# Forming the low parts of the expert weights on GpSimd, between the transfers of the scatter, instead of on VectorE

## The reference, cut to what matters

```python
scores = sigmoid(xt @ gate_w.T)              # 16 experts, 4 groups, best 2 groups, best 4 experts
combine = one_hot(indices) weighted          # token x expert
h1 = einsum('td,eid->tei', xt, W1)
h3 = einsum('td,eid->tei', xt, W3)
g = silu(h1) * h3 * combine[:, :, None]      # inner width 176
y = einsum('tei,edi->td', g, W2)
z = silu(xt @ Ws1.T) * (xt @ Ws3.T) @ Ws2.T  # shared expert, inner width 352
out = x + gb * (y + z)
```

## Time and profile before

| | us |
|---|---|
| median of 3 runs | 1134.69 |
| the profiled execution | 1135.41 |
| its span | 1133.6 |
| PE busy in the span | 907.7 (80%) |
| DVE busy | 763.4 (67%) |
| POOL busy | 660.5 (58%) |
| ACT busy | 561.1 (49%) |

### The profile page before, as it was taken

One profiled execution on the slowest core, in us unless ns is written; L12 is line 12 of the kernel. 1 busy time (PEld: TensorE's weight loads), 2 busy tenths in 40 slices (PEclk: granted clock), 3 DMA queues, 4 the chain that ended last, 5 costly groups with the idle time before them and its releaser, 6 DMA issues.

```text
span 1133.6 us, 20825 instructions
## 1 busy us (share of the span) xinstructions
PE 907.7 (80%) x6980; PEld 759.1 (67%) x6981; DVE 763.4 (67%) x1637; ACT 561.1 (49%) x1054; POOL 660.5 (58%) x631
## 2 busy tenths in 40 slices
PE   4484899999999999999999974431159899999930
PEld 4462578888788888888888764331149799999920
DVE  5655778878878888788788856560037666666657
ACT  1202477777777777777777851110024344444410
POOL 4421478788787777887877763047720045555544
PEclk9696899999999999999999995565559899999975
DMA  5743251233422334223242106523310133334345
GB/s 169 278 154 81 58 155 43 74 66 69 147 53 73 64 77 132 52 73 64 59 140 44 27 1 223 154 75 117 115 37 1 33 115 112 118 114 121 102 173 197
DMA packets 65105, 112.31 MB, mean 99 GB/s; under 512 B 16848, under 2 KB 41815, under 8 KB 63151
## 3 DMA queue, kind: packets, MB, share of 16 engines
q1 hardware_dynamic: 46950, 76.94, 25.2%
q0 software_dynamic: 6912, 17.84, 4.4%
q10 hardware_dynamic: 11168, 16.52, 4.3%
HBM read 45.86 MB, written 41.16 MB: 77 GB/s over the span
## 4 chain that ended last, share of the span: by engine, by line
PE 70%; DVE 11%; issue 7%; POOL 4%; DMA 3%; another core or an unknown queue 3%; ACT 2%; SPq 0%; POOLq 0%; DVEq 0%; ACTq 0%
PE bank L621 12%; PE bank L623 12%; PE bank L622 12%; PE bank L738 9%; PE bank L761 8%; PE bank L974 6%; PE bank L885 2%; PE bank L855 2%; PE bank L946 2%; POOL p_lo L1741 1%; PE bank L715 1%; PE bank L832 1%; DVE h L1469 1%; DMA rows_f<-turns 1%
## 5 line engine op out<-in xcount | busy, mean ns | idle before, releaser
L1741 POOL TENSOR_TENSOR p_lo<-p_f,p_hi 128x512 f16<-128x512 f32 x256 | 312.8, 1228 | 85.4 <-ACT p_f L1526 82.7
L1523 ACT ACTIVATE p_hi<-bank,log_up 128x512 f16<-128x512 f32 x256 | 176.1, 688 | 134.4 <-PE bank L623 133.8
L1165 DVE TENSOR_REDUCE nmax<-bank 128x1 fp32r<-128x512 f32 x256 | 173.9, 686 | 68.5 <-PE bank L738 65.8
L1526 ACT ACTIVATE p_f<-bank,log_up 128x512 f32<-128x512 f32 x256 | 175.2, 684 | 0.9 <-POOL p_lo L1741 0.9
L738 PE MATMUL bank<-qk 128*128 128x512 f32 x256 | 152.5, 599 | 6.1 <-DVE nmax L1165 3.8
L761 PEld LDWEIGHTS bank<-vals,p_hi 128*128 128x128 f16 x2048 | 109.5, 97 | 59.2 <-POOL p_lo L1741 30.5
L1145 DVE TENSOR_TENSOR qk<-rows_f,qk 128x512 fp32r<-128x512 f32 (+1 forms) x128 | 143.4, 1121 | 2.0
L761 PE MATMUL bank<-vals,p_hi 128*128 128x66 f16 x2048 | 138.6, 194 | 3.2 <-POOL p_lo L1741 3.0
L761 PE MATMUL bank<-vals,p_lo 128*128 128x66 f16 x1024 | 121.0, 193 | 0.0
L1719 POOL TENSOR_TENSOR turns<-turns 128x512 f32<-128x512 f32 x64 | 90.3, 1413 | 47.0 <-DVE turns L1139 47.0
L1794 POOL DMA_INDIRECT slots<-h,slot_i x64 | 62.3, 974 | 70.0 <-DVE slot_i L1355 50.8
(11 more groups left out here) (228 smaller groups left out, 2093.6 us busy)
## 6 DMA issues: line engine op xcount, KB each, us to landing
rows_f<-turns SPq DMA_DIRECT2D x64, 256.0 KB, 3.9
slots<-pad ACTq DMA_DIRECT2D x4, 2880.0 KB, 11.2
h<-slots SPq DMA_DIRECT2D x80, 144.0 KB
w_hi<-parts SPq DMA_DIRECT2D x16, 512.0 KB, 7.6
rows_f<-kl_f SPq DMA_DIRECT2D x32, 192.0 KB, 3.1
w_raw<-in_w SPq DMA_DIRECT2D x4, 1408.0 KB, 10.5
h_dram<-h_hl SPq DMA_DIRECT2D x3, 1024.0 KB, 4.9
qk<-lat_st SPq DMA_DIRECT2D x16, 192.0 KB, 3.5
```

The lines of the kernel that those rows point to most:

```text
L1165: dve.tensor_reduce(nmax[:, k % MAXES:k % MAXES + 1], max_bank[q % 2][:], AX_X, ALU.max, negate=True)\
L1523: act.activation(p_hi[:, u % TB, :], score_bank[u % 2][:], ACT.Exp, bias=log_up[:, 0:1], scale=SCALE)
L1526: act.activation(p_f[:, u % 2, :], score_bank[u % 2][:], ACT.Exp, bias=log_up[:, 0:1], scale=SCALE)\
L1741: pool.tensor_tensor(p_lo[:, u % TB, :], p_f[:, u % 2, :], p_hi[:, u % TB, :], ALU.subtract).then_inc(s_pl, 1)
```

## The change

The subtraction that makes `w_lo` of one expert leaves position t of the shared stage on DVE. It now stands in POOL's scatter loop, once per tile, behind the four transfers of tile t, with a wait for `w_h` of at least t + 2. Semaphore `w_l` is raised by POOL instead of DVE. Its final value and the waits on it are as before. Nothing else differs.

```diff
@@ shared_position on DVE
                     dve.tensor_tensor(zg, y_bank[par][:, 0:D], g2, ALU.mult).then_inc(z_zg, 1)
 
-                    dve.wait_ge(w_h, t + 2)
-                    dve.tensor_tensor(w_lo[:, bass.ds(t, 1)].rearrange("p a k n -> p (a k n)"),
-                                      w_raw[:, bass.ds(t, 1)].rearrange("p a k n -> p (a k n)"),
-                                      w_hi[:, bass.ds(t, 1)].bitcast(F32).rearrange("p a k n -> p (a k n)"),
-                                      ALU.subtract).then_inc(w_l, 1)
                     dve.wait_ge(z_zg, t + 1)
@@ the scatter on POOL, for t in range(NT): for r in range(TOPK):
                     pool.indirect_dma_start(slots, bass.IndirectOffsetOnAxis(ap=slot_i[:, t, r:r + 1], axis=0),
                                             h2[:, t, :], None).then_inc(sent, 16)
 
+                pool.wait_ge(w_h, t + 2)
+                pool.tensor_tensor(w_lo[:, t].rearrange("p k n -> p (k n)"), w_raw[:, t].rearrange("p k n -> p (k n)"),
+                                   w_hi[:, t].bitcast(F32).rearrange("p k n -> p (k n)"), ALU.subtract).then_inc(w_l, 1)
+
```

## The result

The changed kernel takes 1100.7 us (median of 4 runs, 1099.97 to 1101.27) against 1134.85 for the kernel before beside it (4 runs, 1134.49 to 1136.28): a ratio of 0.9696, 95% interval 0.968 to 0.9713. The profiled execution took 1101.17 us, its span is 1098.9.

A forecast was written before the change was run, and what follows sets the result against it. Unbroken scatter issue was taken to stall the shared stage and delay the routed experts. Tiles of 4 x 1.27 + 1.75 + 0.3 = 7.13 us start them 27.6 us earlier: 1135.4 - 27.6 = 1107.8, 1107.1 against the median; range 1102 to 1123.

The forecast's parts named there:

- What bounds the kernel: Scatter beside shared stage: unbroken issue, one transfer per 1.27 us, builds a backlog delaying PE's signals and the routed experts.
- rival B: Shared stage: it stands until 838 for a reason other than the scatter; 35.7 us later, 1170; chance 0.04.
- Step 1: Shared stage on DVE: losing 16 x 0.88 us of subtractions gains nothing per position.
- Step 2: Scatter loop on POOL: 16 subtractions of 128x704 at 1.75 us each, bounds 1.69 and 1.95.
- the 1117: Forecast time in us at the upper bounds: 7.75 us per tile on POOL and a slower landing, gaining 17.9 us.
- Step 3: POOL's scatter loop: switching between transfers and subtraction costs 0.3 us per tile, making 7.13 us, bounds 6.9 and 7.75.
- Step 4: Start of the scatter: POOL waits for expert 0's high part; first subtraction at 762.1, bound 768.1.
- Step 5: Scatter: gaps free the shared stage; positions every 4.32 us stay ahead of POOL, stage ends near 830 instead of 899.
- Step 6: Start of routed experts: POOL's last transfer is late next; PE starts at 873.3 instead of 900.90, 27.6 us earlier.
- Contention: POOL beside DVE in the shared stage: POOL standing once per tile for DVE's 0.42 us instruction costs 6 us, 1113.
- A: Scatter: gaps too short, each four transfers still block PE's signals; with full recovery 1153 us; chance 0.09.
- C: Scatter: a milder backlog sometimes makes POOL wait; tiles of 8 to 8.7 us, 1120 to 1131; chance 0.17.

The follow-up runs named there:

- f2: Kernel before plus one POOL subtraction of 128x256, result unused, behind every four transfers; 1092.33 us against 1135.48 for the kernel before.
- e9: Kernel before with all 16 low parts moved to POOL, behind the whole unbroken scatter; 1134.06 us against 1133.2 for the kernel before.
- f4: Kernel before without the routed experts' low parts (products read the high parts twice); 1130.16 us against 1135.48 for the kernel before.
- f1: Kernel before plus one POOL instruction of 128x1 behind every four transfers; 1130.01 us, ratio 0.9957 to the kernel before.
- f3: Changed kernel, but in runs of 16 transfers with four low parts after each; 1111.02 us against 1135.48 for the kernel before.
- r_before: The kernel before, unchanged, run again in a session without the stall; 1074.08 us.
- r_after: The changed kernel, unchanged, run again in a session without the stall; 1101.06 us, ratio 1.0239 to the kernel before.
- e5: Kernel before, but ACT makes all high parts first and POOL 13 low parts during routing, three behind the scatter; 1085.72 us, ratio 1.0103.
- g1: Kernel before plus one POOL subtraction of 128x256 behind every four transfers, in a session without the stall; 1082.65 us, ratio 1.0075.
- e4: Changed kernel, but in runs of 16 transfers with four low parts after each; 1095.12 us against 1074.64 for the kernel before.
- e3: Changed kernel, but expert t - 2's low part stands behind tile t's transfers, the last two behind the scatter; 1092.35 us against 1074.64 for the kernel before.

## Why the prediction was right or wrong

**What bounds the kernel** was right for the session measured, and incomplete. I argued that unbroken issue builds up a backlog that delays PE's signals. With the stall the runs bear out that unbroken issue is needed for it: of what was tried, gaps alone cure it (f2 and the changed kernel against e9 and f4; f1's short ones do little), and a long run brings it back (f3). That what builds up is a backlog is not shown. But the same unbroken issue does no harm in four sessions out of seven. The page, the chain and the windows of one trace could not tell that. None of my rivals was "the stall belongs to the session": rival B came nearest, that the stall isn't the scatter's, and it too had the changed kernel stall on. So the right direction was in part luck: in four sessions of seven the same change loses. With r_before in hand, the forecast would have been two numbers: 3% faster where the stall is, 2% slower where it is not.

**Step 1**, DVE's relief is worth nothing: right with the stall (e9). Without it the relief gives back 7.0 us of transfer time, a term that I had not seen since the transfers of the earlier trace rows are short: in the stall DVE hardly worked beside them.

**Step 2**, 1.75 us for a subtraction: 1.67 to 1.70, so the line between 128x512 and 128x1024 (1.69) was right, and the 0.06 that I added for a busy DVE was not needed. The upper bound of a tile was also added up too high: its terms give 5.24 + 1.95 + 0.5 = 7.69, not 7.75, which is 0.9 us on the 1117.

**Step 3, the switching, is the step that failed.** I put it at 0.3 us per tile on top of four times 1.27, and my lower bound still had 0.13 of it. Measured, the tile is 6.65 = 4 x 1.266 + 1.69 - 0.11: the subtraction begins within 0.01 us of the transfer's end and the next transfer 0.17 after the subtraction, together less than the one pause of 0.30 that they take the place of. I had taken the price from the write-backs, whose idle time is mostly a wait for their marker. So the length of a tile on POOL, P, was 6.65 where I had 7.13 and a bound of 6.9, and 15 tiles make 7.2 us of the 7.75 by which PE started earlier than I said (865.55 on the clock of before, against 873.3).

**Step 4**, the first low part at 762.1: it began at 763.54 - 1.54 = 762.0. **Step 5**, the gaps free the shared stage: right; `w_hi` came at 762.68, 767.02, 771.40 and so on. **Step 6**, POOL is late next, by its last transfer: right. Its last link was mis-sized: from the start of the last low part (863.41) to PE it is 3.68 us, not 4.3. The transfer landed 2.48 us after its issue, as I had said, but the load of the first slots took 2.13 and not 3.1; against that, the transfer left only 1.0 us ahead of the low part (862.43) and not 1.3. That is the rest, 0.6 us. It is where the lower bound had it (3.7); P alone took the time below the range.

**Contention** went the other way than I feared. I asked what would happen if POOL stood still once per tile for DVE's addition. No low part on POOL took over 1.70 us in the changed kernel; it was DVE's addition that stood, five times in 16. The timeline of DVE in the changed kernel:

```profile
772.67 0.43 DVE L1413 TENSOR_TENSOR xa<-xa,msk 128x256 f32<-128x256 f32 x1
776.99 1.86 DVE L1413 TENSOR_TENSOR xa<-xa,msk 128x256 f32<-128x256 f32 x1
...
790.20 1.98 DVE L1413 TENSOR_TENSOR xa<-xa,msk 128x256 f32<-128x256 f32 x1
```

POOL's low parts began at 776.87 and 790.19, just ahead of two of the long ones. It cost nothing, because the shared stage had 37 us to spare.

**The rivals.** A, B and C all needed idle time ahead of POOL's low parts after the first, and there was none. **Without the stall** the price of the change adds up from the same rows. From the first transfer to the landing wait it is 87.8 us in r_before (748.67 to 836.47) and 113.5 in r_after (752.54 to 866.05), 25.7 more. That is 9.2 of first pause, 15 x (6.65 - 5.07) = 23.7 of low parts, less the 7.0 of shorter transfers: 25.9. The medians differ by 25.5.

## What to carry to other kernels

A stretch in which every engine waits for "remote" or "issue" may belong to the session, not to the program: run the unchanged kernel on other chips and at other times before a change is built on that stretch, and price the change for both cases. Work that is put on the engine which issues the transfers is free only while something else is later; once the transfers are what the next stage waits for, each microsecond of it is paid. And before a subtraction is moved from VectorE to GpSimd, look at what the other engine does at that time: a VectorE instruction with two inputs in SBUF (in e5 also some with one) and an ordinary GpSimd instruction wait for each other, in both directions; the issue of a transfer waits for VectorE's subtraction, but not the other way round.

## What the runs showed of the hardware

**A stall that comes and goes with the session.** Where it exists, signals of PE to ACT and DVE arrive late beside a long run of indirect transfers (Silu idle up to 33.3 us), with the clock at 0.53 in the stretch. As far as these rows tell, only PE's signals are late. In the trace of before, an inner product on PE ended at 773.44, and the DVE product for which its Silu must wait besides (L1393, 794.02) at 794.36; the Silu began at 827.30. From ACT to DVE and from DVE back to PE it then takes under 0.1 us each (827.62 to 827.65, 827.99 to 828.05):

```profile
772.95 0.49 PE L623 MATMUL bank<-w_hi,x_hl 128*128 128x352 f32 x1
794.02 0.34 DVE L1393 TENSOR_TENSOR pre<-bank,sl 128x176 f32<-128x176 f32 x1 [14.21 <-issue]
827.65 0.34 DVE L1393 TENSOR_TENSOR pre<-bank,sl 128x176 f32<-128x176 f32 x1 [27.95 <-issue]
828.05 0.66 PE L855 MATMUL bank<-ident,pre 128*88 128x128 f32 x2 [24.04 <-issue]
```

The stall is not tied to the number a chip goes by: sessions 2 and 5 bear one number, 4 and 6 another, and of each pair one stalled. Whether a number stands for the same chip each time, the runs don't tell. A second sign goes with it. The trace records 16 increments as a transfer lands. From 770 to 780 us I count 112 of 112 such records in r_before, 96 of 96 in g1, but 19 of 128 in before, 19 of 128 in e9 and 43 of 86 in the changed kernel's first measurement, which did not stall. Over the whole scatter, 1024 increments, it is 1024 in r_before and in r_after, 198 in before, 666 in the changed kernel's first measurement and 306 in f2. So the missing records mark the session, and the gaps decide whether the program suffers from it. What in the chip does this stays open; no run tells. Nor does any run tell whether the stall is there when nothing is recorded: every run on record has its span and its clock from a recording. The Trainium skill (NOTIFIC — the notification-queue block, section 7.1) says that the block which takes the records of events holds its producers back when its inner queue is full, and that this can throttle an engine; that would fit the late signals, though not by itself the missing records, and no run here can show it.

**Two inputs on VectorE against GpSimd.** Between ordinary instructions, the one that comes second stands. A DVE instruction of 128x256 beside POOL's low part takes 1.5 to 2.0 us in the changed kernel instead of 0.42, while the low part keeps its 1.70; and in g1 a POOL instruction of 128x256 that began at 764.46, 0.11 us behind a low part on DVE, took 1.23 instead of 0.62, while that low part kept its 0.88. A run of POOL instructions is not let go between them: in e4, where four low parts stand one behind the other, DVE's addition stood for all that was left of them and ended 0.30 us behind the last (798.78 + 6.10 = 804.88, against 798.00 + 6.58 = 804.58).

```profile
798.00 6.58 POOL L1789 TENSOR_TENSOR w_lo<-w_raw,w_hi 128x704 fp32r<-128x704 f32 x4
```

```profile
798.78 6.10 DVE L1413 TENSOR_TENSOR xa<-xa,msk 128x256 f32<-128x256 f32 x1
```

In e5, with ten in a row, DVE's instructions did get in, one between two of POOL's; what makes the difference is not shown. Nor do the recorded starts tell the order exactly: in e3 the addition that began at 778.48, 0.13 us ahead of a low part by the records (778.61), stood for it all the same and took 2.10. With the issue of a transfer it goes one way only: beside DVE's low part it takes 1.49 us instead of 0.96, but the low part that began at 763.49 in r_before, in the middle of a transfer's issue, kept its 0.88, and of the 159 low parts and additions on DVE that began so in 16 traces none took over 0.04 us longer. The Trainium skill (SBUF — State Buffer, section "SBUF: two separate sides") calls this an exclusive lock, held for the whole instruction by whoever comes first. For ordinary instructions the trace agrees: DVE's addition at 790.20 ended at 792.18, 0.30 us behind the POOL instruction that had begun 0.01 us before it. The half speed that the prediction cited from the GPSIMD Engine Reference holds as well: 1.69 against 0.88.
